# Five projections of a decoder layer as three float32r passes, with the low halves subtracted on VectorE

## What is computed

```python
x = x + attn(layernorm(x))             # stage A: causal, 16 heads, int8 fake-quantized linears
x = x + xattn(layernorm(x), context)   # stage X: cross attention, 120 keys, softmax1, masked
x = x + ffn(layernorm(x))              # stage F: layer norm, attention of its own, layer norm, router
                                       # then 8 experts, top 2 of 8, capacity 25%
# in X:  q = x @ Wq ; kv = context @ Wkv ; out = attend(q, k, v) @ Wproj + bproj
# in F:  h = layer_norm(x) * ln1_g + ln1_b
#        q = (h @ wq + bq) * 0.25 ; k = h @ wk + bk ; v = h @ wv + bv ; out = attend(q, k, v) @ wo + bo
```

## Time and profile before

| | us |
|---|---|
| median of 3 runs | 5286.25 |
| lowest and highest | 5284.78, 5296.24 |
| profiled execution, its own time | 5298.91 |
| span of the profile, first to last instruction | 5297.2 |
| mean granted TensorE clock | 0.98 of full |

### The profile page before, as it was taken

One profiled execution on the slowest core, in us unless ns is written; L12 is line 12 of the kernel. 1 busy time (PEld: TensorE's weight loads), 2 busy tenths in 40 slices (PEclk: granted clock), 3 DMA queues, 4 the chain that ended last, 5 costly groups with the idle time before them and its releaser, 6 DMA issues. The chain is left out here.

```text
span 5297.2 us, 147856 instructions
## 1 busy us (share of the span) xinstructions
PE 4926.9 (93%) x45659; PEld 4001.1 (76%) x45660; DVE 3899.7 (74%) x9253; ACT 3865.1 (73%) x8215; POOL 2027.2 (38%) x1692
## 2 busy tenths in 40 slices
PE   0999999979999999889999999995799999999998
PEld 0777777758888888667777777773599999899997
DVE  7888888868888888689999999997744444344433
ACT  5899999958888888767777777773655555555554
POOL 1222232313333333234444444442144544444443
PEclk9999999989999999999999999997799999999999
DMA  6777777746666666467777777772432332323222
GB/s 189 184 188 187 190 186 189 187 125 194 196 196 197 196 197 197 138 170 185 186 185 186 183 185 186 185 185 70 52 64 47 63 57 45 64 49 64 47 47 28
DMA packets 631700, 750.63 MB, mean 142 GB/s; under 512 B 143365, under 2 KB 560334, under 8 KB 631472
## 3 DMA queue, kind: packets, MB, share of 16 engines
q1 hardware_dynamic: 575136, 679.62, 49.0%
q0 software_dynamic: 49152, 63.09, 7.3%
q10 hardware_dynamic: 7184, 5.00, 0.3%
HBM read 476.49 MB, written 272.24 MB: 141 GB/s over the span
## 5 line engine op out<-in xcount | busy, mean ns | idle before, releaser
L1762 POOL DMA_INDIRECT out_dram<-exp_gated,exp_token x256 | 419.7, 1639 | 717.6 <-ACT exp_gated L1666 377.1
L1011 DVE TENSOR_REDUCE F_tops<-F_score 128x2 f32<-128x512 f32 x1024 | 668.8, 686 | 22.6 <-PE F_score L706 14.3
L1712 DVE TENSOR_TENSOR exp_hT_lo<-exp_whole,exp_hT_hi 128x512 fp32r<-128x512 f32 x512 | 355.4, 694 | 437.1 <-ACT exp_hT_hi L1655 437.1
L871 ACT ACTIVATE F_probs<-F_scoreT 128x512 f32<-128x512 f32 x1024 | 571.4, 591 | 74.7 <-PE F_scoreT L677 73.4
L1011 DVE TENSOR_REDUCE A_tops<-A_score 128x3 f32<-128x384 f32 x1024 | 526.9, 553 | 83.9 <-PE A_score L696 65.5
L1615 PE MATMUL exp_res<-exp_w_hi,exp_hT_hi 128*128 128x256 f32 x2048 | 573.5, 280 | 0.0
L1617 PE MATMUL exp_res<-exp_w_lo,exp_hT_hi 128*128 128x256 f32 x2048 | 568.0, 277 | 0.0
L1618 PE MATMUL exp_res<-exp_w_hi,exp_hT_lo 128*128 128x256 f32 x2048 | 567.9, 277 | 0.0
L1666 ACT ACTIVATE exp_gated<-exp_y,exp_gate 128x256 f32<-128x256 f32 x256 | 109.4, 498 | 624.1 <-DVE exp_y L1736 594.5
L871 ACT ACTIVATE A_probs<-A_scoreT 128x384 f32<-128x384 f32 x1024 | 463.3, 481 | 17.2 <-PE A_scoreT L665 8.8
L1602 PE MATMUL exp_hid<-exp_xT_hi,exp_w_lo 128*128 128x512 f32 x1024 | 405.9, 396 | 0.0
(11 more groups left out here) (355 smaller groups left out, 14326.1 us busy)
## 6 DMA issues: line engine op xcount, KB each, us to landing
QS<-d_q SPq DMA_DIRECT2D x384, 192.0 KB, 3.7
KS<-d_k SPq DMA_DIRECT2D x256, 192.0 KB, 4.0
QS<-d_q SPq DMA_DIRECT2D x384, 128.0 KB, 3.8
KS<-d_k SPq DMA_DIRECT2D x256, 128.0 KB, 4.0
d_q<-A_q_parts SPq DMA_DIRECT2D x64, 384.0 KB, 3.0
d_k<-A_k_parts SPq DMA_DIRECT2D x64, 384.0 KB, 2.8
QS<-d_q SPq DMA_DIRECT2D x384, 64.0 KB, 3.6
d_q<-X_q_parts SPq DMA_DIRECT2D x64, 384.0 KB, 2.6
```

The lines of the kernel that those rows point to most:

```text
L871: nc.scalar.activation(probs[m][0:KR, at:at + HB, :].rearrange("p u x -> p (u x)"), scoreT[i % TB][0:KR, 0:HB * TCOL], ACT.Exp)\
L1011: nc.vector.tensor_reduce(dst, src, AX.X, ALU.max).then_inc(score_read, 1)
L1712: v.tensor_tensor(hT_lo[:, f, :], whole[f % OB][:, :], hT_hi[:, f, :], ALU.subtract).then_inc(h_split, 1)
L1762: nc.gpsimd.indirect_dma_start(out, bass.IndirectOffsetOnAxis(token[j % (2 * XB)][:, s:s + 1], 0), gated[par][:, s, :], None, bounds_check ...
```

## The change

Five kinds of projections are made of float32r passes: in F q, k, v and proj, in X q and proj. X's k and v, A, and all scores stay as they are. A float32 value a is split into a rounded part a_hi (float32r) and a remainder a_lo = a - a_hi, and a product of a and b becomes a_hi b_hi + a_hi b_lo + a_lo b_hi.

- The rounded parts of `xT` and `aT` are what ACT's copy writes, now into float32r tiles. In F that copy is one plain copy of 128x512 instead of two of 128x256 with scale and bias: ln1_g is multiplied into the weights, and ln1_b goes into the biases, once at the start of F.
- The remainders are new instructions of DVE: it waits for ACT's copy (`x_cast`, `a_cast`), subtracts it from the PSUM bank, and it is now DVE that signals `work_drained` for xT, xT0, xT1 and aT. DVE's lists get the steps xT0, aT and xT1 in X, and xT and aT in F. The lists of the other engines do not change.
- The weights are split once at the start of X (ACT and DVE) and of F (ACT and POOL). PE waits for them before its first q.
- `QS` and `KS` become tiles of each stage; the two constant rows of `KS` are filled by two DMAs (`fill`) at the second turn of each stage. Loads of `prepare` are put in another order, and tiles that only A and X use are freed before F.

```diff
-        "DVE": ("topB v mcopy maxima tok0 tok1 norm maxima maxima maxima maxima topA wo stats maxima var c0 c1 "
+        "DVE": ("topB v mcopy maxima tok0 tok1 norm maxima xT0 maxima aT xT1 maxima maxima topA wo stats maxima var c0 c1 "
...
-        "DVE": ("topB maxima v maxima maxima tok0 tok1 maxima maxima maxima maxima maxima topA stats var maxima "
+        "DVE": ("topB maxima v maxima maxima tok0 tok1 maxima maxima xT maxima aT maxima maxima topA stats var maxima "
...
+                def fill():
+                    for t in KS:
+                        sp.dma_start(t[96:98, :, :], C["minus"][:, 0:KP].unsqueeze(1).broadcast_to([2, H, KP])).then_inc(filled, 16)
...
+                def product(out, rows, columns, start, stop):
+
+                    (a, a_lo), (b, b_lo) = rows, columns
+                    mm(out, a, b, start=start, stop=False)
+                    mm(out, a, b_lo, start=False, stop=False)
+                    return mm(out, a_lo, b, start=False, stop=stop)
...
+                            if kind != "A" and isinstance(g, int) and g == 0:
+                                pe.wait_ge(w_split, len(w_lo))
...
-                            last = nc.scalar.activation(xT[gp][:, int(name[2]), :], W[:, 0:256], ACT.Copy)
+                            nc.scalar.activation(xT[gp][:, int(name[2]), :], W[:, 0:256], ACT.Copy).then_inc(x_cast, 1)
+                            continue
...
-                            for c in range(2):
-                                last = nc.scalar.activation(xT[gp][:, c, :], W[:, c * 256:(c + 1) * 256], ACT.Identity,
-                                                            bias=C["ln1_b"][:, c:c + 1], scale=C["ln1_g"][:, c:c + 1])
+                            nc.scalar.activation(xT[gp][:, :, :], W[:, :].rearrange("p (c t) -> p c t", c=2), ACT.Copy)\
+                                .then_inc(x_cast, 1)
+                            continue
...
+                    dve.wait_ge(shifts, 1)
+                    nc.vector.scalar_tensor_tensor(bias_qk[:, 0, :], work[0][:, 0:2], 0.25, C["bq_f"][:, :], ALU.mult, ALU.add)\
+                        .then_inc(bias_ready, 1)
...
+                        if name in ("xT0", "xT1"):
+                            c = int(name[2])
+                            dve.wait_ge(x_cast, 2 * g + c + 1)
+                            nc.vector.tensor_tensor(xT_lo[gp][:, c, :], W[:, 0:256], xT[gp][:, c, :], ALU.subtract)\
+                                .then_inc(work_drained[bank], 1)
...
+                        if name == "aT":
+                            dve.wait_ge(a_cast, g + 1)
+                            nc.vector.tensor_tensor(aT_lo[:, :, :], W[:, :].rearrange("p (c t) -> p c t", c=2), aT[:, :, :],
+                                                    ALU.subtract).then_inc(work_drained[bank], 1)
...
+                if kind == "F":
+                    pool.wait_ge(bias_ready, 4)
+                    for i in range(3):
+                        for c in range(2):
+                            nc.gpsimd.tensor_scalar(C["wF"][i][:, c, :], C["wF"][i][:, c, :], C["ln1_g"][:, c:c + 1], None, ALU.mult)\
+                                .then_inc(w_scaled, 1)
+                    for i in range(4):
+                        pool.wait_ge(w_high, i + 1)
+                        nc.gpsimd.tensor_tensor(w_lo[i][:, :, :], C["wF"][i][:, :, :], w_hi[i][:, :, :], ALU.subtract)\
+                            .then_inc(w_split, 1)
```

155 lines of the change are left out of this document (110 added, 45 removed).

## The result

| | before | after |
|---|---|---|
| median, us | 5287.1 | 5556.8 |
| lowest and highest, us | 5284.8, 5296.2 | 5552.1, 5561.8 |
| profiled execution, its own time | 5298.9 | 5559.2 |
| stage X, first to last instruction | 1099.6 | 1329.9 |
| stage F | 1423.8 | 1462.0 |

The changed kernel is slower by a factor of 1.0507 (95% interval 1.0489 to 1.0525). The forecast was 5472 us in a range of 5340 to 5600. The time lies in the range, but at the place of the clock rival (5555), not at that of the likeliest case. Of the 260 us between the two profiled executions X has 230 and F 38.

What follows compares the result with a forecast made beforehand. F was taken as full on TensorE and VectorE, X as TensorE-bound with one VectorE hole. X +147, F +32 and starts +7 made +186 us: 5485 on the profiled time, 5472 against the median, range 5340 to 5600.

Steps and rivals of the forecast that it cites:

- the clock rival: TensorE's pauses between xT and q lower its clock each turn of X: +83 us, 5555 us (5510 to 5620); chance 0.29.
- the likeliest case: Whole kernel: X +147, F +32, starts +7 us, giving 5472 us, own range 5400 to 5510; chance 0.43.
- The chain: In X, banks given back by VectorE delay aT, yT and q: score reduce 2.72 us late, turn +2.55 us.
- X's start: X's first q waits for two weight casts and two subtractions in VectorE's queue: about +1.5 us.
- the 0.25 us that VectorE was to get back from GpSimd: In X's turn, GpSimd's sum blocks VectorE's rounding of y for less time: 0.25 us back, leaving +2.3 us a turn.
- The signs: X's profile: TensorE waits about 2 us for aT's bank, VectorE 1.2 before aT's remainder, 1.5 before q's reduce.
- TensorE's gain: Three float32r passes save 0.32 us a projection: 0.63 us a turn in X, 1.26 in F, 121 us in all.
- F's turns: In F, VectorE's queue grows by 1.22 us, less 0.41 and 0.3: +0.5 us a turn, +32 us in all.
- F's start: F's first q waits for small matmuls, bias operations, scalings and subtractions on GpSimd: +4 to +6 us.
- Small loss: VectorE's hole hides most of X's bank waits: X +0.3 to +0.9, F 0 to 0.8, 5306 to 5381 us; chance 0.19.
- Faster: In X and F, TensorE's 121 us arrive, VectorE's new work lies in blocked or idle time: 5172 us; chance 0.05.
- The passes at float32's pace: Projections in X and F run at 0.216 us a record, not 0.118: 2.6 us each, over 5600; over 5620 had 0.02.

## Why the prediction was in range and its likeliest case was not

The parts against the forecast, in the profiled executions' own times:

| part | forecast, us | measured, us | from |
|---|---|---|---|
| X, chain (and its start) | +148.5 | +160.2 | X with TensorE kept busy, less before |
| X, clock | 0 (rival: +83) | +70.1 | after, less X with TensorE kept busy |
| F, turns and start | +37.5 | +38.2 | stage F |
| the rest of the span | 0 | -8.2 | A and what follows F; no part of the change, as said above |
| sum | +186 | +260.3 | |

**The chain** was walked rightly. Counted from the V copy, aT was to start at +5.24 and started at +5.14, the aT remainder at +6.76 and 6.55, q at +7.93 and 7.63, the score matmul at +9.34 and 9.16, the reduce behind it at +9.76 and 9.59. The reduce is thus 2.55 us later than before, for 2.72. From there to the next V copy it is 9.47 us, exactly as before, where I had taken off a hole of 0.17. The two errors cancel: 16.51 + 2.55 = 19.06, which is the turn without a fall. X's start was forecast at +1.5 us; the first V copy came 4.7 us later in the stage than before (46.8 for 42.1).

The step that failed inside the chain is the 0.25 us that VectorE was to get back from GpSimd. The rounding of y took 1.14 us in this turn, as before; over the stage its mean went from 1.10 to 1.11 us. It did come back where its place changed: in the version with the earlier remainder it takes 0.48 us, behind GpSimd's sum instead of beside it. Over 64 turns the 0.25 us are 16 us, more than the 12 by which X, chain and start, was low. The blocked time hangs on the place in VectorE's queue; that TensorE is less loaded did not move it.

**The signs** asked for in X came: TensorE's wait ahead of aT, about 2 us forecast, is 113.4 us over 64 turns, 1.8 a turn; VectorE's ahead of aT's remainder is 0.89 in the shown turn, for 1.2, and the one ahead of the reduce 1.45, for 1.5:

```profile
L877 PE MATMUL X_work<-ident_f,X_tok 128*128 128x128 f32 x256 | 44.1, 297 | 113.4 <-DVE X_xT_lo L1096 112.0 <-DVE X_tok L1220 1.3
L1104 DVE TENSOR_TENSOR X_aT_lo<-X_work,X_aT 128x512 fp32r<-128x512 f32 x64 | 44.3, 692 | 56.5 <-ACT X_aT L1020 56.5
```

The sign asked for in F, TensorE waiting for reduces, did not come: over the stage it waits 6.8 us for them, less than for xT's remainder (15.9) or for the V copy (13.9).

**The clock** is the step that put the likeliest case 85 us off. Its price was nearly right: 1.3 us a turn forecast, 1.45 measured in a turn like the one shown (20.32 less 18.87 of the same kind), and 70 us in the stage for 83, because about one turn in twelve has no fall and the turns behind it lose less. What failed was the weighing, 0.29 against 0.43. The walk itself gave the two pauses (aT waits for the bank, yT for aT's), and the argument that they are short, split, and followed by dense matmuls was set against the earlier trace rows, where 4.01 busy of 6 us had been followed by 0.50. The stretch ahead of the fall after the change was busy for a like share, 4.63 of 7.38; a stretch with 4.57 of 7.38 had no fall behind it, so such a row does not settle a single turn. Rows of before with a pause of this size in X's steady turn did not exist, and the only row near it spoke for the fall; it should have had the larger chance.

**TensorE's gain** was put a little high. q in passes takes 1.53 us up to the score matmul (1543.77 to 1545.30), where in float32 it took 1.80: 0.27, not 0.32, since the first of the twelve steps is 0.22 us and only the others 0.118. And with the bank's chain out of the way X shows just 0.27 a turn of the two projections' gain (16.29 to 16.02), F 0.73 of the four.

**F's turns** were forecast at +0.5 us and came at +0.46 (21.71 less 21.25; 21.84 less 21.35 in steady turns). The number is right partly by luck, since the parts differ: I put all of it on VectorE's queue (+1.22, less 0.41 of a hole, less 0.3 of blocked time), but of the price about two fifths is the bank. q's start was said to be within 0.1 us of its place; TensorE's own rows have 15.9 us of waiting, 0.25 a turn, for the xT remainder in front of q (the group holds q and k; the wait is at q), and VectorE 13.6 us for ScalarE's copy:

```profile
L666 PE MATMUL F_work<-F_xT,F_w_hi 128*128 128x256 f32 x512 | 158.5, 310 | 15.9 <-DVE F_xT_lo L1100 15.9
...
L1100 DVE TENSOR_TENSOR F_xT_lo<-F_work,F_xT 128x512 fp32r<-128x512 f32 x64 | 43.6, 682 | 13.6 <-ACT F_xT L992 13.6
```

**F's start** was mis-sized, +4 to +6 forecast and +8.8 measured (first q 19.8 us into the stage, 11.0 before):

```profile
2475.40 1.89 POOL L1264 TENSOR_SCALAR c_fq<-c_fq,c_ln_g 128x256 f32<-128x256 f32 x2 [18.14 <-DVE F_bias_v L1062]
2477.28 1.82 POOL L1264 TENSOR_SCALAR c_fk<-c_fk,c_ln_g 128x256 f32<-128x256 f32 x2
2479.08 1.93 POOL L1264 TENSOR_SCALAR c_fv<-c_fv,c_ln_g 128x256 f32<-128x256 f32 x2
2481.75 1.26 POOL L1268 TENSOR_TENSOR F_w_lo<-c_fq,F_w_hi 128x512 fp32r<-128x512 f32 x1 [0.74 <-ACT F_w_hi L916]
...
2485.42 1.27 POOL L1268 TENSOR_TENSOR F_w_lo<-c_fo,F_w_hi 128x512 fp32r<-128x512 f32 x1
```

The scalings took 0.94 us each (5.64 for six), where half of a 128x512 sum had been the estimate (0.65), and GpSimd could not begin before 2475.40, 8.3 us into the stage, because the small matmuls and bias operations go first. The four subtractions, 1.26 each, were right.

**The rivals.** Small loss is out: the banks' chain closed. Faster would have needed it absent, and even without any remainder the gain is 0.95% (5240.7), not the 5172 us it was priced at: it took TensorE's relief as arriving in full. The small loss's own terms, 0.9 and 0.8 us over 64 turns, add up to 109 us and not to the 95 of its upper end. The passes at float32's pace are out.

## What to carry to other kernels

When a PSUM bank is shared by a chain of steps, who gives it back can matter more than how long the work is: in X the same 1.2 us of VectorE work cost nothing when no bank and no projection waited for it, 2.7 us a turn when they waited for VectorE's place in its queue, and 1.2 when that place was earlier. In F, where VectorE has no such hole, the work itself was the larger part (0.67 of 1.08). Walk the bank's chain through every queue before trusting busy shares, and put the instruction that gives the bank back as far ahead as its input allows. Where the walk gives TensorE pauses in every turn, weigh a fall of its clock by runs like these, and price it at the work that lies behind the pause: here 1.88 and 0.68 us a turn had a fall in eleven of twelve turns, 0.29 and 0.60 had none.

## What the hardware showed that I had not expected

- The falls of the clock repeat. In the steady part of X after the change one turn in twelve has no fall. Two turns later the fall lasts 6.8 us, twice as long as the others, and that turn takes 21.7 us; then the falls begin at places that creep from 5.2 to 7.5 us behind the V copy, until a turn has none. A mean turn hides three kinds of turns, and one shown alone can mislead.
- Idle matmuls are worth their price: zeros multiplied in TensorE's pauses, nine and four a turn, made the kernel 75 us faster.
- The rounding of y took 1.1 us in its old place and 0.48 one instruction further back in the queue, with the same data. The Trainium skill (SBUF — State Buffer, section "Who interferes with whom") has this as an exclusive hold of a pair of ports that VectorE's fast modes and GpSimd share; the runs agree, with 0.49 us as the mean in the one order and 1.11 in the other:

```profile
L1135 DVE TENSOR_SCALAR X_grid<-X_yin,yinv 128x512 f32<-128x512 f32 x64 | 31.3, 489 | 4.0 <-DMA X_yin<-d_y 4.0
L1135 DVE TENSOR_SCALAR X_grid<-X_yin,yinv 128x512 f32<-128x512 f32 x64 | 70.9, 1107 | 5.6 <-DMA X_yin<-d_y 5.5
```

The first row is the version with the earlier remainder, the second the changed kernel. GpSimd's sum in the two (the first again is the earlier remainder's):

```profile
1510.25 1.29 POOL L1293 TENSOR_TENSOR X_xb<-X_xin,c_bo_a 128x512 f32<-128x512 f32 x1 [0.27 <-DVE X_tok L1220]
1538.28 1.30 POOL L1293 TENSOR_TENSOR X_xb<-X_xin,c_bo_a 128x512 f32<-128x512 f32 x1 [0.27 <-DVE X_tok L1220]
```

It ends at 1511.54, and the rounding starts at 1511.49; in the changed kernel it runs to 1539.58, over most of the rounding (1538.73 to 1539.87). The subtraction at 1511.15, PSUM and SBUF in, took its usual 0.43 us beside the sum. VectorE gained 0.6 us a turn by the order, which may be part of why that version lost so much less; no run tests that alone.
